# A mixture-of-experts decoder layer on one core: expert outputs added into one row per token, in place of two rows that are summed later

## The reference, cut to what matters

```python
gate_scores = softmax(einsum('btd,ed->bte', x, Wg))
topk_val, topk_idx = top_k(gate_scores, 2)
comb = (one_hot(topk_idx, E) * (topk_val / sum(topk_val))[..., None]).sum(-2)
for e in range(E):
    a, b = split(einsum('btd,hd->bth', x, W1[e]) + b1[e], 2)
    g = a * sigmoid(b)
    eo = einsum('bth,dh->btd', g, Wo) + bo
    out = out + eo * comb[..., e:e + 1]
```

## Time and profile before

| | us |
|---|---|
| median of 3 runs (lowest, highest) | 1426.19 (1421.7, 1429.67) |
| the profiled execution, its time | 1429.21 |
| its span, first to last instruction | 1427.4 |
| attention, until the last chosen rows are scattered | 0 to about 840 |
| experts, first load of a tile to last scatter | 844 to 1259 |
| last stage | 1264 to 1427 |

### The profile page before, as it was taken

One profiled execution on the slowest core, in us unless ns is written; L12 is line 12 of the kernel. 1 busy time (PEld: TensorE's weight loads), 2 busy tenths in 40 slices (PEclk: granted clock), 3 DMA queues, 4 the chain that ended last, 5 costly groups with the idle time before them and its releaser, 6 DMA issues.

```text
span 1427.4 us, 30146 instructions
## 1 busy us (share of the span) xinstructions
PE 1276.7 (89%) x7734; PEld 900.9 (63%) x7735; DVE 1147.2 (80%) x3145; ACT 743.8 (52%) x1740; POOL 641.3 (45%) x978
## 2 busy tenths in 40 slices
PE   6888899999989999999988659999999999968886
PEld 4443556555555565555554448888888888858786
DVE  0457688988889889889887658888888888859998
ACT  1226677777777777777776312222222222214444
POOL 3002244554445545554544433333333333348886
PEclk9999999999999999999999769999999999989999
DMA  7646476775765756757655764433344433379995
GB/s 176 139 97 112 121 152 147 165 174 139 161 143 142 160 140 151 147 143 161 132 132 193 291 225 135 134 128 131 132 134 134 134 129 130 132 268 335 329 340 190
DMA packets 182817, 237.57 MB, mean 166 GB/s; under 512 B 21376, under 2 KB 144256, under 8 KB 176960
## 3 DMA queue, kind: packets, MB, share of 16 engines
q1 hardware_dynamic: 158864, 169.50, 47.2%
q0 software_dynamic: 17488, 55.02, 10.2%
q10 hardware_dynamic: 6368, 11.89, 2.4%
HBM read 138.34 MB, written 98.30 MB: 166 GB/s over the span
## 4 chain that ended last, share of the span: by engine, by line
PE 61%; DVE 16%; issue 8%; DMA 6%; ACT 4%; POOL 2%; SPq 2%; DVEq 0%; ACTq 0%; POOLq 0%
PE psO L617 6%; PE psHb L1390 5%; PE psHb L1387 5%; PE psHb L1386 5%; PE psS L724 5%; PE psHa L1386 4%; PE psHa L1387 4%; PE psHa L1390 4%; PE psB L646 4%; PE psT L734 4%; DVE negmax L1022 3%; DVE x2in L1582 3%; DMA qstack<-q_parts 3%; PE psO L568 2%; PE psX L1410 2%
## 5 line engine op out<-in xcount | busy, mean ns | idle before, releaser
L1022 DVE TENSOR_REDUCE negmax<-psS 128x2 f32<-128x512 f32 x512 | 349.7, 687 | 83.6 <-PE psS L724 66.1
L863 ACT ACTIVATE probs<-psT 128x512 f32<-128x512 f32 x512 | 303.2, 598 | 159.7 <-PE psT L734 144.1
L1467 ACT ACTIVATE sig<-hb 128x512 f32<-128x512 f32 x135 | 85.4, 632 | 287.0 <-DVE hb L1540 283.3
L724 PE MATMUL psS<-kstack,qstack 96*128 96x256 bf16 x1024 | 195.4, 273 | 37.6 <-DVE kstack L1120 13.4
L734 PE MATMUL psT<-qstack,kstack 99*128 99x512 bf16 x512 | 194.1, 381 | 4.6 <-ACT probs L863 4.5
L1349 POOL DMA_INDIRECT g_rows<-g,slot x135 | 134.4, 995 | 70.0 <-issue 66.7
L724 PEld LDWEIGHTS psS<-kstack,qstack 96*128 96x128 bf16 x1024 | 92.5, 104 | 94.0 <-DVE negmax L1022 36.5
L477 POOL DMA_INDIRECT lists<-x,slots x128 | 128.3, 1003 | 33.9 <-issue 30.1
L617 PE MATMUL psO<-probs,vaug 128*32 128x512 f32 x1024 | 138.4, 613 | 0.4 <-ACT probs L863 0.4
L1551 DVE SCALAR_TENSOR_TENSOR g<-g,xe,sig 128x512 f32<-128x512 f32 x135 | 101.5, 752 | 26.1 <-DVE g L1547 16.4
L1540 DVE TENSOR_TENSOR hb<-psHb,b 128x512 f32<-128x512 f32 x135 | 93.4, 692 | 32.2 <-issue 28.8
(11 more groups left out here) (207 smaller groups left out, 2953.2 us busy)
## 6 DMA issues: line engine op xcount, KB each, us to landing
rows<-g_rows SPq DMA_DIRECT2D x32, 1024.0 KB, 8.0
qstack<-q_parts SPq DMA_DIRECT2D x192, 128.0 KB
xe<-lists SPq DMA_DIRECT2D x135, 133.0 KB, 2.1
q_parts<-qpart SPq DMA_DIRECT2D x32, 384.0 KB
sums<-x SPq DMA_DIRECT2D x32, 264.0 KB
x2in<-sums SPq DMA_DIRECT2D x32, 264.0 KB, 4.9
xt<-in_x_t SPq DMA_DIRECT2D x32, 256.0 KB
part_raw<-in_f_t SPq DMA_DIRECT2D x32, 256.0 KB, 5.1
```

The costliest lines, as they stand in the source:

```text
L724: last = mm(psS[:, u % 2, hh * S:(hh + 1) * S], qstack[0:KROWS, b1.s4, 2 * hp + hh, c * P:(c + 1) * P], kstack[0:KROWS, b1.s4, :], start=T ...
L863: nc.scalar.activation(probs[:, u % PT, :], psT[:, u % 2, :], ACT.Exp, scale=SELF_SCALE).then_inc(sm["exp_done"], 1)
L1022: v.tensor_reduce(negmax[:, b1.s2, 2 * hp:2 * hp + 2, c], psS[:, u % 2, :].rearrange("p (h k) -> p h k", h=2), AX.X, ALU.max, negate=True) ...
```

## The change

`g_rows` has one row per token. The scatter of g adds to what is there instead of writing, so the row number no longer depends on which of the two experts it is. The buffer must be zero first: SP stores zeros from a small tile over all of it, in three portions at the end of steps 0, 1 and 2. The weight parts of steps 1 and 2 move to steps 3 to 5, those of 17 and 18 to 19 to 21, and the first rounding waits until the rows are cleared. Two scatters must not add to the same row at once: tile n's scatter waits for the three scatters before it where its expert is another than tile n-1's (a table `turn`), and always in tiles 1 to 7. There are eight `xe` buffers, and the loops go by eight tiles. `place` copies the row number in place of `away`. In the last stage one row per token is loaded, and `row_sum` goes.

```diff
-    ROW = D + E + 2
+    ROW = D + E + 1
...
-        if n in (1, 17):
-            return range(n - 1, n + 1)
-        return range(n, n + 1) if 2 <= n < 16 or 18 <= n < 32 else range(0)
+        if n in (3, 4, 5, 19, 20, 21):
+            first = 2 * (n % 16 - 3) + n // 16 * 16
+            return range(first, first + 2)
+        return range(n, n + 1) if 6 <= n < 16 or 22 <= n < 32 else range(0)
...
+        def clear_rows(t):
+            places = dram["g_rows"].rearrange("(p k) h -> p k h", p=P)
+            pieces = places.shape[1] // ZROWS
+            if t.n == 0:
+                sp.wait_ge(dram["zeros_made"], 1)
+            for n in range(t.n * pieces // 3, (t.n + 1) * pieces // 3) if t.n < 3 else ():
+                sp.dma_start(places[:, n * ZROWS:(n + 1) * ZROWS, :],
+                             zeros[:, :].unsqueeze(1).to_broadcast([P, ZROWS, zeros.shape[1]])
+                             ).then_inc(dram["rows_cleared"], 16)
...
             store_parts(t)
+            clear_rows(t)
...
             if k == 0:
                 act.wait_ge(dram["pads_stored"], 32)
+                act.wait_ge(dram["rows_cleared"], 16 * (dram["g_rows"].shape[0] // (P * ZROWS)))
...
-                v.tensor_copy(x2[:, b6.s2, :, D + E + 1], topf[:, b6.s2, :, 0]).then_inc(sm["comb_ready"], 1)
+                last.then_inc(sm["comb_ready"], 1)
...
-                wait(sp, "g_ready", done(t.back(4)))
+                wait(sp, "g_ready", done(t.back(8)))
...
-            wait(sp, "rows_added", done(t.back(4), QC))
+            wait(sp, "g_transposed", done(t.back(4), QC))
...
             o = t.back(2)
+            turn = None
+            for m in range(1, 4):
+                before = o.back(m)
+                if active(o) and (not o.fixed or o.n >= 8):
+                    turn = pool.value_load(turn_tab[0:1, bass.ds(o.n, 1)], min_val=0, max_val=16) if turn is None else turn
+                    wait(pool, f"g_stored{before.s4}", ring(before) + turn)
+                elif active(o) and before.n >= 0:
+                    wait(pool, f"g_stored{before.s4}", ring(before) + 16)
+            if active(o):
+                wait(pool, "g_ready", done(o))
             if active(t):
-                wait(pool, f"xe_loaded{t.s4}", ring(t) + 16)
-                wait(pool, "g_ready", done(o))
-                pool.tensor_tensor(away[:, t.s4:t.s4 + 1], xe[:, t.s4, FIRST:FIRST + 1],
-                                   expf[:, bass.ds(t.n, 1)], ALU.subtract).then_inc(sm["away_ready"], 1)
+                wait(pool, f"xe_loaded{t.s8}", ring8(t) + 16)
+                pool.tensor_tensor(place[:, t.s4:t.s4 + 1], xe[:, t.s8, ID:ID + 1], zero[:, :], ALU.add
+                                   ).then_inc(sm["place_ready"], 1)
...
                 pool.indirect_dma_start(out=dram["g_rows"], out_offset=bass.IndirectOffsetOnAxis(
-                    ap=slot[:, o.s4:o.s4 + 1], axis=0), in_=g[:, o.s4], in_offset=None
+                    ap=slot[:, o.s4:o.s4 + 1], axis=0), in_=g[:, o.s4], in_offset=None, compute_op=ALU.add
                     ).then_inc(sm[f"g_stored{o.s4}"], 16)
...
-                for c in range(QC):
-                    wait(pool, "g_transposed", QC * t.n + c - 3)
-                    pool.tensor_tensor(row_sum[:, t.s2 * QC + c], rows[:, t.s4, c, 0:H], rows[:, t.s4, c, H:2 * H], ALU.add
-                                       ).then_inc(sm["rows_added"], 1)
...
-                    wait(pe, "rows_added", QC * t.n + c + 1)
+                    if c == 0:
+                        wait(pe, f"rows_loaded{t.s4}", ring(t) + 16)
...
-                wait(dve, "away_ready", done(i))
+                wait(dve, "place_ready", done(i))
                 wait(dve, f"g_stored{i.s4}", ring(i))
-                v.scalar_tensor_tensor(slot[:, i.s4:i.s4 + 1], away[:, i.s4:i.s4 + 1], 0.0, xe[:, i.s4, ID:ID + 1],
-                                       ALU.not_equal, ALU.add)
+                v.tensor_copy(slot[:, i.s4:i.s4 + 1], place[:, i.s4:i.s4 + 1])
...
-            "g_rows": nc.dram_tensor("g_rows", (2 * (T + 2 * E * P), H2 // 2), F32, kind="Internal").ap(),
+            "g_rows": nc.dram_tensor("g_rows", (T + 2 * E * P, H2 // 2), F32, kind="Internal").ap(),
```

More of the change, by code:

```diff
@@ L70, in s4, with n, s8, back @@
         return self.r % 4
+class Tile(Step):
+    @property
+    def n(self):
+        return 8 * self.j + self.r
+    @property
+    def s8(self):
+        return self.r % 8
+    def back(self, k):
+        return Tile(self.j, self.r - k)
 def attention(nc, ctx, io, dram):
@@ L112, in attention @@
     rden = sb("rden", [P, 2, QC * 8])
-    with nc.sbuf_tensor("pad", [P, 2 * E, ROW], F32) as pad:
+    ZROWS = 4
+    with nc.sbuf_tensor("pad", [P, 2 * E, ROW], F32) as pad, nc.sbuf_tensor("zeros", [P, dram["g_rows"].shape[1]], F32) as zeros:
         pass
@@ L1176, in experts @@
     ROW = dram["lists"].shape[1]
-    ID, FIRST = D + E, D + E + 1
+    ID = D + E
     STRIDE = dram["stride"]
@@ L1189, in experts @@
     I32 = mybir.dt.int32
-    rows, row_sum, x2in, y, result = (dram[k] for k in ("rows", "row_sum", "x2in", "y", "result"))
+    rows, x2in, y, result = (dram[k] for k in ("rows", "x2in", "y", "result"))
     w1_hi, w1_lo, b1, bo = dram["w1_hi"], dram["w1_lo"], dram["b1"], dram["bo"]
@@ L1206, in experts @@
         pass
+    with nc.sbuf_tensor("g", [P, 4, H], F32) as g:
+        pass
     past = sb("past", [P, TILES, E])
@@ L1219, in experts @@
     xet_lo = sb("xet_lo", [P, 2, DC * P], F32R)
-    away = sb("away", [P, 4])
+    place = sb("place2", [P, 4])
+    zero = sb("zero", [P, 1])
     slot = sb("slot", [P, 4], U32)
@@ L1265, in pipeline @@
     def pipeline(eng, step):
[L1267 to L1273, removed]
+        for r in range(16):
+            step(Tile(0, r))
+        with eng.Fori(2, TILES // 8) as j:
+            for r in range(8):
+                step(Tile(j, r))
+        for r in range(TILES % 8 + 3):
+            step(Tile(TILES // 8, r))
     def pair_pipeline(eng, step):
@@ L1346, in step @@
+            if active(o):
+                wait(pool, "g_ready", done(o))
+            if active(t):
+                wait(pool, f"xe_loaded{t.s8}", ring8(t) + 16)
+                pool.tensor_tensor(place[:, t.s4:t.s4 + 1], xe[:, t.s8, ID:ID + 1], zero[:, :], ALU.add
+                                   ).then_inc(sm["place_ready"], 1)
+            elif active(o):
+                pool.tensor_tensor(place[:, o.s4:o.s4 + 1], xe[:, o.s8, ID:ID + 1], zero[:, :], ALU.add)
             if active(o):
-                if not active(t):
-                    wait(pool, "g_ready", done(o))
@@ L1641, in decoder_layer @@
             place("w1_hi", [P, W1], F32R)
-            with (nc.sbuf_tensor("rows", [P, 4, QC, 2 * H], F32) as rows, nc.sbuf_tensor("row_sum", [P, 4, H], F32) as row_sum,
+            with (nc.sbuf_tensor("rows", [P, 4, QC, H], F32) as rows,
                   nc.sbuf_tensor("x2in", [P, 4, QC, D + E], F32) as x2in, nc.sbuf_tensor("y", [P, 4, QC, D], F32) as y):
-                dram.update(rows=rows, row_sum=row_sum, x2in=x2in, y=y)
+                dram.update(rows=rows, x2in=x2in, y=y)
             place("w1_lo", [P, W1], F32R)
```

55 lines of the change are left out of this document (32 added, 23 removed).

## The result

The changed kernel takes 1463.46 us (median of four runs, 1462.11 to 1470.67) beside 1427.93 for the kernel before: a ratio of 1.0258, 95% interval 1.0223 to 1.0292. It is slower, by 35.5 us and not by 9.4. The profiled execution has 1463.09 us and a span of 1461.2, 33.8 above the span of before.

| stretch | before, us | after, us | difference | forecast |
|---|---|---|---|---|
| start to first scatter | 855.66 | 903.72 | +48.1 | +34.9 |
| first to last scatter | 403.76 | 416.33 | +12.6 | +4.6 |
| last scatter to the first load of rows | 4.28 | 7.08 | +2.8 | +1 |
| that load to the end | 163.7 | 134.1 | -29.6 | -31.1 |

What follows compares the result with a forecast made beforehand. TensorE was taken to bound the experts, VectorE the last stage, with room in the first three steps' DMA. Terms 34.9 + 1 - 1 + 4.6 + 1 - 5.8 - 24.3 - 1 = +9.4 gave 1435.6 us; range 1407 to 1468.

Steps and rivals of the forecast that it cites:

- the likeliest case: Whole kernel: all terms as worked out, +9.4 us to 1435.6, spanning 1420 to 1449; chance 0.56.
- Rival (b): Expert stage: the accumulate lands late, at 7 us costing 37 in place of 4.6, so 1468 us; chance 0.14.
- Rival (c): Last stage: slow bias comes from transfers into x2in, not POOL, so -24.3 is lost: 1460 us; chance 0.10.
- The clears: Steps 1 to 3: xt queued behind the clears makes TensorE wait 9.1, 13.9 and 11.9 us, sum +34.9.
- The upper bound of 47: Upper bound for the clears' cost in us, at the 314 GB/s that the last stage averages.
- Rival (a): First three steps: the clears find room, the three waits together staying under 18 us; 1410 us, faster; chance 0.20.
- The weight parts: Attention steps: first three moved parts enter busy steps, +1 us (0 to 4); second three cost nothing.
- The serial scatters: Expert stage, tiles 1 to 7: waits for landings of 3.4 us make periods of 4.2; +4.6 us (0 to 16.4).
- the upper bound of 5.1: Expert stage: upper bound in us for an adding scatter's landing, 4.14 and another 1.0 for a second pass.
- The last scatter: End of the expert stage: the last scatter lands 1.0 us later, +1.
- The last stage: Bias faster without POOL's row_sum, a pair 3.80 us instead of 4.70 (-24.3); start -5.8, tail -1.
- the dropped copy: Copy of the first expert, dropped: saves 0.06 us 32 times, at most 2 us, taken as -1.

Runs made afterwards that it cites:

- kernel with plain scatters: Changed kernel with scatters that write instead of adding, all waits and rows kept, one expert's outcome per row left out; measured 1450.10 us.
- the additions put back: Changed kernel with two 128x512 POOL additions a pair put back in the last stage, on tiles that lie still, row loads kept half size; measured 1488.58 us.
- two other executions: Changed kernel with scatters that write instead of adding, with the clears (1450.10 us) and without the clears and the waits for them (1403.65 us).

## Why the prediction was right in direction and wrong in size

The direction held, and 1463 lies inside 1407 to 1468, but the likeliest case (1420 to 1449) does not hold it. That the range does is luck: its upper end came from rivals (b) and (c), and neither came about. The waits were where the prediction had them; two of its terms were too small, one cost it left out (the lower clock of TensorE behind a wait), and one it put at nothing (steps 19 to 21 with two weight parts each).

**The clears: +34.9 forecast, 46.4 measured.** The three waits were put at 9.1, 13.9 and 11.9; they were 10.45, 16.24 and 13.35, 5.1 us more. The rate of 382 GB/s is not to blame: while the engines were full, the rate was 378 GB/s in step 1 (28.0 to 53.2 us), 383 in step 2 (78.5 to 99.7) and 406 in step 3 (125.7 to 145.4). Nor is it that xt is issued late, since the engines stay full from its issue until it lands. What the step had wrong in part is where the next qstack loads come: in steps 2 and 3 they are issued 3.9 and 7.3 us later than worked out (70.54 and 117.74 against 66.6 and 110.4), the projections, without their waits, only 2.4 and 5.9 later. That is 1.5 us of each of these waits; the other 2.1 us stay open.

What the step left out altogether is TensorE's clock: after each wait the projection ran at the lower level, 3.78 us for 1.89. From the place of step 1's projection to the projection of step 4, before the change and after (same columns as above):

```profile
42.90:123.82 80.92, 66.27 (x283) 33.57 (x281) 44.12 (x78) 25.87 (x53) 6.58 (x6) 0.95 0.59 129
```

```profile
42.90:169.13 126.23, 70.88 (x286) 36.32 (x284) 43.71 (x76) 25.25 (x52) 6.58 (x6) 0.80 0.71 217
```

The stretch is 45.3 us longer: TensorE is idle 40.7 us more (55.35 against 14.65), nearly all of it for xt, and busy 4.6 us more with the same work. The kernel with plain scatters, with the same attention stage, comes to 45.7 there by another division: 36.7 us of waits for xt, and 8.5 us more of busy time.

The upper bound of 47 is 49 by the working's own rate of 314 GB/s. Rival (a), that the clears find room, is out as the change has them, though spread over 15 steps and a few lines further up it is true: I asked whether the engines had room in the three steps, not where in a step the queue had.

**The weight parts: +1 forecast**, within 0 to 4, of which the second three were to cost nothing. It is the second three that cost: 2.9 us in steps 17 to 22, a wait of 1.5 us for VectorE in each step with two parts, three such steps in place of one. What the first three cost beside the clears the runs don't separate.

**The serial scatters: +4.6 forecast, 12.6 measured.** The step that failed is the price of the landing, 3.4 us, made of a plain scatter's 2.4 and one more pass of 1.0. The adding scatter lands after 4.8 to 5.2, near the upper bound of 5.1; it also holds POOL for 1.56 us, which the step had at 1.0. The 2.4 was already too low: it was read off the end of the data's movement, and a plain scatter lands after 2.8 to 3.9. The other way, the 0.68 from POOL's small operation to the scatter is 0.34 in this stretch (914.80 to 915.14). With plain scatters the same waits leave the stage at 1.5 us above before, so the error lies in the price of adding. The formula (seven periods above 3.01, less 3.7 of slack) gives 7 x (5.36 - 3.01) - 3.7 = 12.7 with the measured period, but that it meets 12.6 is chance: the kernel without these waits is 10.6 us shorter in this stage. By the eighth scatter the waits had cost 15.6 us (37.53 us after the first, against 21.96 there), and the later tiles gave back 5.0, not 3.7; the other 2.0 us of the 12.6 remain without the waits. Rival (b) needed a landing of 6 us. The changes of expert cost TensorE nothing, as forecast: POOL waited 80.8 us for landings in the stage, yet behind tile 8 TensorE is busy 355.00 of 355.00. Only the last of these waits costs 0.9 us, as no work of TensorE is left to cover it.

**The last scatter: +1 forecast, +2.8 measured**, the same error in part. The chain of waits has

```profile
1320.05 6.95 DMA g_rows<-g,slot
```

where the earlier trace rows had 4.14, and 4.33 is what the kernel with plain scatters has. But the adding scatter lands after some 5 us elsewhere. The last three start only 1.95 us apart here, after the wait for the one before them, so part of the 6.95 can be the two ahead; no run separates that.

**The last stage: -31.1 forecast, -29.6 measured.** The bias fell to 0.87 a pair, TensorE became the full engine, and a pair takes 3.79 us where 3.80 was forecast. Rival (c), the transfers, is excluded by the additions put back, which gave the 4.7 us again with the small loads.

Together, 1.7 + 46.4 + 12.6 + 2.8 - 29.6 = +33.9, the 33.8 us of the spans. The 1.7 is what is left of the attention stage's 48.1. The 2.9 of the weight parts and the dropped copy are in it, but it can't be divided further: the 46.4 comes from two other executions, and two with the same attention stage end it 1.1 us apart.

## What to carry to other kernels

A bulk transfer is priced by the load that has to come through while it is under way, above all the one behind it in its queue, and not by the room that the engines have in the mean: the same 20 clears cost 48.8 us just ahead of a late load and nothing some lines further up, where the queue's next instruction waits anyway. Another queue alone did not do it: with all 20 at once there, 24.9 of the 48.1 us stayed. A wait of a nearly full TensorE can cost more than its length, as the work behind it here started at the lower clock: spread over 15 steps, 29.0 us more of idle time came with 17.8 us more of busy time. An adding scatter has its own price, so measure its landing before anything is made to wait for it; waits that only some data need are better made to depend on the data.

## What was not expected of the hardware

- The adding scatter of 128 rows of 2 KB takes 1.56 us on POOL where the writing one takes 0.99, lands after 4.8 to 5.2 us where the other lands after 2.8 to 3.9, and in the expert stage fills 0.85 of the engines' time at 133 GB/s, where writing fills 0.40 at 131, before the change as in the kernel with plain scatters (945 to 1300 us).
- SP's time to issue a transfer depends on what is already under way: six qstack loads take 2.8 us, and 7.60 beside the clears on POOL's queue (from 19.92 us); six clears, eight times as large each, take 18.19, and one xt behind them 2.50 where it took 0.45.
- After each of the three waits for xt TensorE ran the eight matmuls of the projection in 3.78 us, which took 1.89 before, with a granted clock of 0.50 in the stretch ahead.
